# Gate logits in plain fp32 column strips, with turns, softmax and staging moved in expert 0

## What is computed

```python
h = jax.nn.relu(jnp.einsum('bi,eio->beo', x, eW1) + eb1)      # 8 experts, 1024 -> 1024
h = jax.nn.relu(jnp.einsum('beh,eho->beo', h, eW2) + eb2)     # 1024 -> 512
expert_out = jnp.einsum('beh,eho->beo', h, eW3) + eb3         # 512 -> 256
gates = jax.nn.softmax(jnp.einsum('bi,tie->bte', x, gW) + gb, axis=-1)   # 2 tasks x 8 experts
tin = jnp.einsum('bte,bed->btd', gates, expert_out)
th = jax.nn.relu(jnp.einsum('btd,tdh->bth', tin, tW1) + tb1)
th = jax.nn.relu(jnp.einsum('bth,tho->bto', th, tW2) + tb2)
out = jax.nn.sigmoid(jnp.einsum('bth,tho->bto', th, tW3) + tb3)
```

## Time and profile before

| what | value |
|---|---|
| median of 3 runs | 585.0 us (584.58 to 585.32) |
| the profiled execution's own time | 584.63 us |
| its span in the profile | 582.9 us |
| granted TensorE clock | 1.00 |
| matmul records of PE | 3315 |
| transfers | 63.27 MB, mean 109 GB/s |

### The profile page before, as it was taken

The page is one execution under the profiler, slowest core; times in us unless marked ns, Lnnn a source line. Parts: engine busy times, 40 slices in busy tenths (PEclk is TensorE's granted clock), DMA queues, the critical chain, the costliest instruction groups (busy, mean ns, idle before and its releaser), DMA issues.

```text
span 582.9 us, 9215 instructions
## 1 busy us (share of the span) xinstructions
PE 575.5 (99%) x3315; PEld 505.0 (87%) x3315; DVE 464.5 (80%) x591; ACT 265.2 (46%) x336; POOL 44.2 (8%) x46
## 2 busy tenths in 40 slices
PE   9999999999999999999999999999999999999998
PEld 6888888888999889988999889998899889998776
DVE  7954199895998859996799859987698959988492
ACT  3545175333654264441745255451644336543553
POOL 0000010012000300003000300003000120004000
PEclk9999999999999999999999999999999999999999
DMA  8340334225223422316122432315141252235100
GB/s 310 134 144 12 133 112 143 75 65 224 72 72 108 179 73 94 122 36 252 48 96 72 158 130 72 115 65 187 65 144 72 70 218 72 72 118 170 36 0 2
DMA packets 23277, 63.27 MB, mean 109 GB/s; under 512 B 1617, under 2 KB 6865, under 8 KB 19682
## 3 DMA queue, kind: packets, MB, share of 16 engines
q1 hardware_dynamic: 21906, 58.64, 28.4%
q0 software_dynamic: 1216, 4.23, 2.2%
q10 hardware_dynamic: 144, 0.26, 0.1%
HBM read 63.08 MB, written 0.04 MB: 108 GB/s over the span
## 4 chain that ended last, share of the span: by engine, by line
PE 92%; DVE 4%; issue 2%; ACT 1%; DVEq 0%; ACTq 0%
PE psum L277 24%; PE psum L279 24%; PE psum L278 24%; PE psum L418 12%; PE psum L420 6%; DVE w_lo L780 1%; DVE scratch L816 1%; PE psum L501 1%; PE psum L375 1%; DVE h_lo L791 0%; PE psum L478 0%; PE psum L477 0%; DVE scratch L822 0%; DVE scratch L868 0%; ACT w_hi L735 0%
## 5 line engine op out<-in xcount | busy, mean ns | idle before, releaser
L277 PE MATMUL psum<-h_hi,w_hi 128*128 128x512 f32 (+1 forms) x340 | 131.9, 388 | 0.8 <-DVE h_lo L791 0.8
L278 PE MATMUL psum<-h_lo,w_hi 128*128 128x512 f32 (+1 forms) x340 | 131.7, 387 | 0.0
L279 PE MATMUL psum<-h_hi,w_lo 128*128 128x512 f32 (+1 forms) x340 | 131.7, 387 | 0.0
L780 DVE TENSOR_TENSOR w_lo<-w_raw,w_hi 128x1024 fp32r<-128x1024 f32 (+1 forms) x79 | 111.2, 1427 | 10.5 <-ACT w_hi L588 8.1
L791 DVE SCALAR_TENSOR_TENSOR h_lo<-scratch,h_hi 128x512 fp32r<-128x512 f32 (+1 forms) x68 | 61.7, 910 | 47.1 <-ACT scratch L673 34.9
L277 PE MATMUL psum<-t_both,w_hi 128*128 128x256 f32 x336 | 95.4, 284 | 1.6 <-DVE scratch L874 1.6
L279 PE MATMUL psum<-t_both,w_lo 128*128 128x256 f32 x336 | 95.2, 283 | 0.0
L278 PE MATMUL psum<-t_both,w_hi 128*128 128x256 f32 x336 | 95.1, 283 | 0.0
L619 ACT ACTIVATE w_hi<-w_raw 128x1536 fp32r<-128x1536 f32 x28 | 41.8, 1494 | 80.7 <-PE psum L279 39.5
L277 PEld LDWEIGHTS psum<-h_hi,w_hi 128*128 128x128 f32 x340 | 63.9, 188 | 14.0 <-DVE h_lo L791 1.2
L279 PEld LDWEIGHTS psum<-h_hi,w_lo 128*128 128x128 f32 x340 | 63.9, 188 | 13.0
(11 more groups left out here) (104 smaller groups left out, 807.7 us busy)
## 6 DMA issues: line engine op xcount, KB each, us to landing
w_raw<-eW_pairs SPq DMA_DIRECT2D x28, 1024.0 KB, 4.8
w_raw<-eW SPq DMA_DIRECT2D x40, 512.0 KB, 3.7
scratch<-gates_dram POOLq DMA_DIRECT2D x8, 512.0 KB, 3.9
w_raw<-eW_first SPq DMA_DIRECT2D x7, 512.0 KB, 6.2
w_raw<-tW SPq DMA_DIRECT2D x4, 512.0 KB, 3.6
scratch<-xT SPq DMA_DIRECT2D x7, 256.0 KB, 6.2
w_raw<-eW_first SPq DMA_DIRECT2D x2, 256.0 KB, 4.0
scratch<-xT ACTq DMA_DIRECT2D x1, 256.0 KB, 3.3
```

The source lines that it names most:

```text
L277: pe.matmul(bank, weights_hi, moving_hi, start=first, stop=False)
L278: pe.matmul(bank, weights_hi, moving_lo, start=False, stop=False)
L279: return pe.matmul(bank, weights_lo, moving_hi, start=False, stop=last)
L780: dve.tensor_tensor(wide(w_lo, slots), raw, wide(w_hi, slots).bitcast(F32), ALU.subtract).then_inc(slot_ready, 1)
```

## The change

The gates' logits no longer use split halves. gw is a buffer of its own of eight tiles of 32 columns, 16 of them the weights and 16 zeros, in plain fp32. Contraction tile k is multiplied with the raw x_raw tile and goes to column strip k mod 4 of the array, and so to one of four groups of 32 partitions of bank 4: eight matmuls in the place of 16. They stand before tile 6 of group 0. DVE copies the bank to `turned` at once, all 128 partitions, and group 1's tiles for bank 4 wait for that copy.

`turn_logits` stands before k = 4 of group 1 and turns whole squares of 128 by 128; a tensor_reduce adds the four strips and the bias comes after. `turn_gates` stands before k = 6 of group 1. The softmax on DVE and ACT moves ahead of the second-layer splits.

The differences of x are written to t_raw, a region of their own, so x_raw stays as it was loaded until the logits are done; then the staging of all eight hidden tiles uses its eight places and waits for nothing else. Layer 2's first eight tiles come in another order, so that banks of group 1 taken last are needed later. The parameters' load is issued one weight unit earlier, ahead of x6 and x7. POOL's memset of task_in waits for expert 0's hidden low halves too.

```diff
-BANK_LOGITS, BANK_GATES = 0, 1
+BANK_LOGITS, BANK_TURNED, BANK_GATES = 4, 0, 1
+STRIP = 32
+STRIPS = P // STRIP
...
+        t_raw = scratch[:, KX * BATCH:2 * KX * BATCH].rearrange("p (k b) -> p k b", k=KX)
...
-        gw = h2_hi[:, 0:2, :].rearrange("p a b -> p (a b)").rearrange("p (k n) -> p k n", k=KX)
+        gw = sb("gw", [KX, STRIP])
...
-                if j == KX // 2 - 1:
+                if j == KX // 2 - 2:
                     sp.dma_start(prm[:], small).then_inc(small_landed, DMA)
...
-            def first_group(g, ks):
+            def first_group(g, ks, between):
                 for k, m in by_tile(ks, MG):
                     j, kk = g * (KX // 2) + k // 2, k % 2
+                    if m == 0 and (g, k) in between:
+                        between[g, k]()
+                    if k == 0 and BANK_HIDDEN1[g * MG + m] == BANK_LOGITS:
+                        pe.wait_ge(logitsT_ready, 1)
...
+                if first:
+                    order[0:2 * MG] = [(0, 0), (0, 1), (1, 0), (1, 1), (0, 2), (0, 3), (1, 2), (1, 3)]
...
             def gate_logits():
-                pe.wait_ge(gw_ready, 3)
-                pe.wait_ge(h1_staged, 1)
+                pe.wait_ge(gw_ready, 2)
+                pe.wait_ge(x_ready, KX)
                 for k in range(KX):
-                    pe.matmul(banks[BANK_LOGITS][:], gw[:, k, :], x_hi[:, k, :], start=(k == 0), stop=False)
-                    mm = pe.matmul(banks[BANK_LOGITS][:], gw[:, k, :], x_lo[:, k, :],
-                                   start=False, stop=(k == KX - 1))
+                    at = k % STRIPS * STRIP
+                    mm = pe.matmul(banks[BANK_LOGITS][at:at + STRIP, :], gw[:, k, :], x_raw[:, k, :],
+                                   start=(k < STRIPS), stop=(k >= KX - STRIPS), tile_position=(0, at))
                 mm.then_inc(logits_done, 1)
...
-                    mm = pe.transpose(banks[BANK_LOGITS][:, b * n:(b + 1) * n],
-                                      turned[0:n, b * P:(b + 1) * P], ident[0:n, 0:n])
+                    mm = pe.transpose(banks[BANK_TURNED][:, b * P:(b + 1) * P], turned[:, b * P:(b + 1) * P], ident[:])
...
-            first_group(0, range(1, KX))
-            first_group(1, range(KX))
-            gate_logits()
-            layer2(0, between=[turn_logits, turn_gates])
+            between = {(0, 6): gate_logits, (1, 4): turn_logits, (1, 6): turn_gates}
+            first_group(0, range(1, KX), between)
+            first_group(1, range(KX), between)
+            layer2(0)
...
-                if m < 2:
-                    act.wait_ge(t_ready, NX)
-                else:
-                    act.wait_ge(h1_ready, m - 1)
-                act.activation(stage[:, m % 2, :], bank[:], ACT.Identity, bias=bias).then_inc(h1_staged, 1)
+                if m == 0:
+                    act.wait_ge(logits_done, 1)
+                    act.wait_ge(x_sum, NX)
+                act.activation(x_raw[:, m, :], bank[:], ACT.Identity, bias=bias).then_inc(h1_staged, 1)
...
             pool.wait_ge(t_ready, NX)
+            pool.wait_ge(h1_ready, K2)
```

More of the change, by code:

```diff
@@ L425, in pair, with layer2 @@
                     mm.then_inc(slot_used, 1)
-            def layer2(e, between=None):
+            def layer2(e):
                 first = isinstance(e, int)
                 order = by_tile(range(0, 6), MG) + by_bank(range(6, 8), MG)
-                for i, (n, m) in enumerate(order):
+                if first:
+                    order[0:2 * MG] = [(0, 0), (0, 1), (1, 0), (1, 1), (0, 2), (0, 3), (1, 2), (1, 3)]
+                for n, m in order:
                     k = ORDER2[n]
@@ L451, in layer2 @@
                         mm.then_inc(slot_used, 1)
-                    if between is not None and i in (len(order) // 4, 3 * len(order) // 4):
-                        between.pop(0)()
             def layer3(done, last):
@@ L602, in t_cast @@
                 place = X_SUMS[n][2]
-                act.activation(block_of(t_hi, *place), block_of(x_raw, *place), ACT.Copy).then_inc(t_hi_ready, 1)
+                act.activation(block_of(t_hi, *place), block_of(t_raw, *place), ACT.Copy).then_inc(t_hi_ready, 1)
             def pair_free(e, i, u):
@@ L690, in _ @@
             first_hi(7)
+            act.wait_ge(soft, 4)
+            act.activation(gate[:], logit[:], ACT.Exp).then_inc(exp_done, 1)
             first_w2_hi(0)
@@ L794, in first_h1_lo @@
                 dve.wait_ge(h1_staged, m + 1)
-                relu_lo(h1_lo[:, :, m, :], halved(stage[:, m % 2, :]), h1_hi[:, :, m, :]).then_inc(h1_ready, 1)
+                relu_lo(h1_lo[:, :, m, :], halved(x_raw[:, m, :]), h1_hi[:, :, m, :]).then_inc(h1_ready, 1)
             def hidden2_lo(done, m):
@@ L929, in sum_x @@
                     dve.wait_ge(x_sum, n)
-                dve.tensor_tensor(block_of(x_raw, *place), block_of(x_raw, *a), block_of(x_raw, *b),
+                dve.tensor_tensor(block_of(t_raw, *place), block_of(x_raw, *a), block_of(x_raw if n < 2 else t_raw, *b),
                                   ALU.subtract).then_inc(x_sum, 1)
@@ L935, in split_t @@
                 place = X_SUMS[n][2]
-                dve.tensor_tensor(block_of(t_lo, *place), block_of(x_raw, *place),
+                dve.tensor_tensor(block_of(t_lo, *place), block_of(t_raw, *place),
                                   block_of(t_hi, *place).bitcast(F32), ALU.subtract).then_inc(t_ready, 1)
@@ L940, in _ @@
             dve.memset(ones[:], 1.0).then_inc(ones_ready, 1)
-            dve.memset(gw.bitcast(F32), 0.0).then_inc(gw_ready, 1)
+            dve.memset(gw[:], 0.0).then_inc(gw_ready, 1)
             half = MG * P
@@ L955, in _ @@
                 first_lo(j)
+            dve.wait_ge(small_landed, DMA)
+            dve.wait_ge(gw_ready, 1)
+            dve.tensor_copy(gw[:, :, 0:T * E], prm_of("gw", 0, KX * T * E).rearrange("p (k n) -> p k n", k=KX)) \
+                .then_inc(gw_ready, 1)
             first_lo(4)
@@ L958, in _ @@
                 sum_x(n)
+            dve.wait_ge(logits_done, 1)
+            dve.tensor_copy(turned[:], banks[BANK_LOGITS]).then_inc(logitsT_ready, 1)
             for n in range(NX):
@@ L973, in _ @@
             first_lo(7)
[L974 to L979, removed]
             wide_gate = [P, BT * T, E]
-            dve.wait_ge(logits_done, 1)
-            dve.tensor_copy(turned[0:2 * T * E, :], banks[BANK_LOGITS][0:2 * T * E, :]).then_inc(logitsT_ready, 1)
             dve.wait_ge(logits_turned, 1)
-            two = banks[BANK_LOGITS][:, 0:BT * 2 * T * E].rearrange("p (b h n) -> p b h n", b=BT, h=2)
+            strips = banks[BANK_TURNED].rearrange("p (b g n) -> p b n g", b=BT, g=STRIPS)[:, :, 0:T * E, :]
             flat = logit[:].rearrange("p (b t) e -> p b (t e)", b=BT)
-            dve.tensor_tensor(flat, two[:, :, 0, :], prm_of("gb", 0, BT * T * E).rearrange("p (b n) -> p b n", b=BT),
+            dve.tensor_reduce(flat, strips, AX.X, ALU.add).then_inc(soft, 1)
+            dve.wait_ge(soft, 1)
+            dve.tensor_tensor(flat, flat, prm_of("gb", 0, BT * T * E).rearrange("p (b n) -> p b n", b=BT),
                               ALU.add).then_inc(soft, 1)
-            dve.wait_ge(soft, 1)
-            dve.tensor_tensor(flat, flat, two[:, :, 1, :], ALU.add).then_inc(soft, 1)
             dve.wait_ge(soft, 2)
@@ L1002, in _ @@
                               ALU.mult).then_inc(gates_ready, 1)
+            first_w2_lo(0)
             dve.wait_ge(gates_turned, 1)
             dve.tensor_copy(turned[0:T * E, :], banks[BANK_GATES][0:T * E, :]).then_inc(gated_ready, 1)
+            first_w2_lo(1)
+            for m in range(MG, 2 * MG):
+                first_h1_lo(m)
+            first_w2_lo(2)
+            first_w2_lo(3)
             with dve.Fori(1, E) as e:
```

11 lines of the change are left out of this document (1 added, 10 removed).

## The result

The changed kernel takes 580.12 us in the median (579.84 to 580.62), the kernel before beside it 584.99 (584.58 to 585.32): a ratio of 0.9918, 95% interval 0.9901 to 0.9935. It is 4.87 us faster, where 2.57 were forecast. The profiled executions stand 4.51 us apart, 584.63 and 580.12; the 0.36 us between the two figures is the kernel before's profiled execution, which lies that much under its median.

A forecast was written before the change was run, and what follows sets the result against it. PE, busy 99% of the span, was taken as the bound, with its waits for DVE in expert 1. Terms -3.62 + 4.17 + 0.05 - 3.17 = -2.57 us gave 582.4 us by the median; range 580.0 to 585.6.

The forecast's parts named there:

- the debt: Expert 1's stalls from DVE running late after the late gate turn; claimed to vanish, -3.17 us, at the least -1.0.
- the likeliest case: Logits in strips: passes issue in program order, 9 steps of 0.43 us; time 582.4 us, chance 0.47.
- rival A: Logits in strips: all four strips run at once, 1.72 + 0.3 us; time 580.3 us, chance 0.21.
- Old logits: Before layer 2: 16 fp32r matmuls leave PE's path, where PE waits nowhere, -3.62 us.
- New logits: Ahead of tile 6 of group 0: eight plain fp32 matmuls in strips enter PE's queue, +4.17 us (1.7 to 9.7).
- The drain: At the strip matmuls: entering and leaving the strips costs 0.3 us, two drains of about 0.16; lower bound 0 if hidden.
- PE's waits at tile 6 and bank 4: Group 0's tile 6 and the copied bank 4: parameters and DVE's work arrive in time, so PE waits 0 us.
- Turns: Two sets of four transposes moved into group 1: +0.05 us for both (-0.1 to +0.35).
- Layer 2's start: Layer 2 directly behind group 1: ACT's staging of banks comes in time under the new order, 0 us, at worst 0.3.
- Rival D: Expert 1: only 1.0 us of its loss is recovered, another step still delaying DVE; 584.6 us, no change, chance 0.07.
- B: Logits in strips: no overlap, 6.88 + 0.3 us; sum +0.4, time 585.4 us, chance 0.17.
- C: Logits in strips: each pass waits for the previous drain, 9.44 + 0.3 us; 588.0 us, chance 0.08 with other losses.

## Why the prediction was right, and where it wasn't

The direction was right, and so were the old logits' price and the debt, the two steps that make the gain. The time lay in the range, near its lower end, but the likeliest case had the mechanism of the new logits wrong and forecast little more than half of the gain, 2.57 of 4.87 us. That the range held the result is due to rival A, whose price it took in, and not to the reasoning of the likeliest case. With the measured 2.06 in the place of 4.17 the prediction's own sum is -4.68 us, 579.95 by the profiled execution, where 580.12 were measured. By its own steps:

- **Old logits, -3.62.** Right: they stood in the open. The same 16 matmuls cost 3.63 in the new place.
- **New logits, +4.17.** The step that failed: "9 steps x 0.43 = 3.87. I take this one, as all rows of PE here start in the program's order." Rows of an undivided array say nothing on this. With four strips it is 4 rounds, 1.72, and some 0.3 for entering and leaving, 2.06 measured. The prediction had named a cost under 2.5 us as a sign that it is wrong, and that sign came. The 0.43 of a pass was right, as was the 0.3. The strips filled in pairs refute the argument that a second pass blocks the passes behind it. Case A had this price, with a chance of 0.21.
- **The drain.** The lower bound of 0 was wrong and the taken value right, by the run without strips.
- **PE's waits at tile 6 and bank 4, 0.** Right: none is in the list of waits.
- **Turns, +0.05.** -0.13 measured. I held the square's weights to be dearer than those of 32 rows. They aren't: the set with 128 columns of weights costs 0.45, the one with 16 costs 0.44.
- **Layer 2's start, 0.** Right to within 0.07 us, and only by the new order, which is worth 0.94 us by the trace of the run in the old one.
- **The debt, -3.17.** Right to the hundredth in the profile: expert 1 now takes expert 2's 38.64. Putting the turned gates and their copy back alone brings 41.80 and 3.06 us again. Rival D is refuted.
- **The start.** The sum has no term for it; tile 2 came 0.22 later in the trace, and the parameters' load in its old place gave no lower time.
- **Rivals B and C.** One strip shows what B would have been, 585.37 against 585.4 worked out. C, with its 9.7 us, falls by the 2.06 of the changed kernel, in which the strips change from pass to pass; in one strip too the passes follow each other by 0.43 and not 0.59.

From the rows before, A and the main case could not be told apart by anything but a rule. The Trainium skill's "TensorE: Matmul & The Clock Gate", "Packing small matmuls", has starts and ends in program order; in these traces passes start in rounds across matmuls, whoever orders them, so that rule does not give the time here. Its table's speedup pointed the right way: the estimate from it was 2.2 us, and 1.72 us of passes and 2.06 with entering and leaving were measured.

What stays open is where the rounds are made: whether the passes stand in PE's queue matmul by matmul and are overtaken there, or are already laid out in rounds. The records don't tell.

## What to carry to other kernels

Where one pass of a loop loses time that the next doesn't, subtract the two stretches between the same instructions: that gave 3.17 us to the hundredth, while the idle column showed 2.0, because it counts neither the end of the matmul before the wait, which otherwise overlaps, nor a slow first step after it. Then look in the late engine's queue for a small copy that waits for PE ahead of work that could run. And if matmuls with few output columns have to be done in plain fp32, divide the array: here the four passes of each strip counted, not the sixteen of all.

## What the runs showed of the hardware that I had not expected

- Four column strips of plain fp32 take the time of one strip's own passes: 16 passes in 1.72 us, against 6.87 us undivided. It made no difference whether neighbouring matmuls went to the same strip (2.08) or to different ones (2.06).
- A division of the array costs 0.31 us for entering and leaving in one strip, and some 0.35 with four strips, once: a second set of sixteen passes added 1.70 us, no more than its rounds.
- Where PE waits, the loss can be two and a half times the idle time that the profile names: with layer 2 in its old order 0.47 us at each late bank, of which 0.19 show as idle. The rest is the 0.16 by which a record (0.39) outlasts a step (0.23), lost when the next matmul can't overlap it, and a first step of 0.34 in place of 0.23.
